# Transposes of new rows one quarter later, products with values two chunks at a time, GpSimd's second rstd before its normalising

## The reference, cut to what matters

```
a = layernorm(x)                                   # per row
q, k, v = a Wq^T, a Wk^T, a Wv^T                   # split into 16 heads of 32
p = softmax(q k^T / sqrt(512) + adj + adj)         # per block and head, 128 x 128
x = x + (p v) Wo^T
b = layernorm(x)
s = softmax(max(b gate_W + gate_b, 1e-4))          # 8 experts, the best two are kept
x = x + sum over the two of weight * (b expert_W[e] + expert_b[e]) / 2
```

## Time and profile before

| what | value |
|---|---|
| median of three executions | 1838.23 us |
| the profiled execution, its own time | 1835.63 us |
| its span in the trace | 1833.7 us |
| TensorE busy | 1658.2 us (90%) |
| VectorE busy | 1277.4 us (70%) |
| ScalarE busy | 985.6 us (54%) |
| GpSimd busy | 985.3 us (54%) |
| TensorE's mean granted clock | 0.96 of full speed |

### The profile page before, as it was taken

The page is one execution under the profiler, slowest core; times in us unless marked ns, Lnnn a source line. Parts: engine busy times, 40 slices in busy tenths (PEclk is TensorE's granted clock), DMA queues, the critical chain, the costliest instruction groups (busy, mean ns, idle before and its releaser), DMA issues. The chain is left out here.

```text
span 1833.7 us, 43506 instructions
## 1 busy us (share of the span) xinstructions
PE 1658.2 (90%) x11856; PEld 1394.6 (76%) x11856; DVE 1277.4 (70%) x4692; ACT 985.6 (54%) x3116; POOL 985.3 (54%) x1722
## 2 busy tenths in 40 slices
PE   4699999999999999999999999998457899999996
PEld 3588788888788887888887888886345678888885
DVE  3467878888878888778888778877543455555554
ACT  3477776677766777766777767767301111111111
POOL 1144555565555555555655555656514456565555
PEclk9899999999999999999999999998669999999998
DMA  5876777777877867777767778766389988888876
GB/s 179 248 212 186 229 230 231 224 236 210 236 229 231 248 201 232 237 224 227 235 202 238 228 228 230 228 201 190 121 278 257 256 163 174 163 166 162 169 157 110
DMA packets 205692, 385.40 MB, mean 210 GB/s; under 512 B 22288, under 2 KB 30480, under 8 KB 205328
## 3 DMA queue, kind: packets, MB, share of 16 engines
q1 hardware_dynamic: 152416, 271.00, 50.3%
q0 software_dynamic: 29680, 69.55, 18.6%
q10 hardware_dynamic: 23360, 42.08, 7.5%
HBM read 206.26 MB, written 176.30 MB: 209 GB/s over the span
## 5 line engine op out<-in xcount | busy, mean ns | idle before, releaser
L593 ACT ACTIVATE prob<-prob,nmax 128x128 f32<-128x128 f32 x1024 | 398.1, 393 | 151.8 <-DVE amax L734 143.7
L983 POOL TENSOR_TENSOR prob<-prob,rinv 128x512 f32<-128x512 f32 x256 | 261.7, 1042 | 254.4 <-DVE rinv L751 254.4
L730 DVE CUSTOM_DVE_ANT_0 prob<-ps_s,bias 128x128 f32<-128x128 f32 x1024 | 237.3, 287 | 163.1 <-PE ps_s L460 117.2
L1190 POOL DMA_INDIRECT out<-yt,token x135 | 211.5, 1566 | 216.0 <-DMA out<-yt,token 72.5
L1126 ACT ACTIVATE xgT_hi<-ps_x 128x512 fp32r<-128x512 f32 x135 | 80.8, 598 | 409.2 <-PE ps_x L1098 330.0
L1110 PE MATMUL ps_y<-we_hi,xgT_hi 128*128 x540 | 227.1, 420 | 21.7 <-DVE xgT_lo L1145 12.3
L1112 PE MATMUL ps_y<-we_hi,xgT_lo 128*128 x540 | 214.8, 398 | 0.0
L1111 PE MATMUL ps_y<-we_lo,xgT_hi 128*128 x540 | 214.6, 397 | 0.0
L631 ACT ACTIVATE pT<-ps_t 128x512 f32<-128x512 f32 x256 | 150.5, 588 | 111.0 <-PE ps_t L469 110.8
L593 ACT ACTIVATION_READ_ACCUMULATOR prob<-prob,nmax 128x1 f32 x1024 | 195.0, 190 | 0.0
L734 DVE TENSOR_REDUCE amax<-prob 128x4 f32<-128x512 f32 x256 | 175.7, 686 | 8.9
(11 more groups left out here) (151 smaller groups left out, 4439.8 us busy)
## 6 DMA issues: line engine op xcount, KB each, us to landing
ks<-kq_parts SPq DMA_DIRECT2D x192, 256.0 KB, 4.3
qs<-kq_parts SPq DMA_DIRECT2D x192, 256.0 KB, 5.5
xg<-x_lists ACTq DMA_DIRECT2D x135, 260.5 KB, 3.6
xin<-x SPq DMA_DIRECT2D x64, 256.0 KB, 6.9
kq_parts<-kT_hi SPq DMA_DIRECT2D x32, 512.0 KB
kq_parts<-kT_lo SPq DMA_DIRECT2D x32, 512.0 KB
kq_parts<-qT_hi SPq DMA_DIRECT2D x32, 512.0 KB
kq_parts<-qT_lo SPq DMA_DIRECT2D x32, 512.0 KB
```

What stands on the lines that cost most here:

```text
L593: last = nc.scalar.activation(prob[:, r, c, h, :], prob[:, r, c, h, :], ACT.Exp, bias=nmax[:, r, i:i + 1], scale=-1.0, accum_out=rsum[:, r ...
L730: last = nc.vector.tensor_tensor_reduce(out=prob[:, r, c, h, :], in0=ps_s[c % 2][:, P * h:P * h + P], in1=bias[:, b % 4, :], scale=-1.0, s ...
L983: tt(prob[:, r, q], prob[:, r, q], rinv[:, r, HC * q:HC * q + HC].unsqueeze(2).to_broadcast([P, HC, P]), ALU.mult)\
L1190: pool.indirect_dma_start(out=out, out_offset=bass.IndirectOffsetOnAxis(ap=token[:, m, :], axis=0), in_=yt[:, r, :], in_offset=None, compu ...
```

## The change

Three edits, all in the order of work of phase A. No operation is added or removed.

1. `small(t, c)`: the transposes of new rows (`X`, parts 0 and 1) of an odd turn stand in quarters 1 and 2 instead of 0 and 1. TensorE, ScalarE and VectorE all follow it.
2. TensorE's `times_v`: instead of one chunk in every quarter, two chunks in quarters 0 and 2 and none in quarters 1 and 3.
3. GpSimd: in an odd turn `second_rstd(t - 3)` stands ahead of `normalise(t, 0)` instead of behind it.

```diff
         def small(t, c):
-            if t % 2 and c < 2:
-                return ("X", t // 2 + 2, c) if okp(t // 2 + 2) else None
+            if t % 2 and c in (1, 2):
+                return ("X", t // 2 + 2, c - 1) if okp(t // 2 + 2) else None
...
                     if ok(t):
                         scores(t, c)
-                    b, cc = (t - 1, c - 1) if c else (t - 2, DC - 1)
-                    if ok(b):
-                        times_v(b, cc)
+                    b, half = (t - 1, 0) if c else (t - 2, 2)
+                    if c % 2 == 0 and ok(b):
+                        times_v(b, half)
+                        times_v(b, half + 1)
                     if ok(t - 1):
                         transpose_probs(t - 1, c)
...
                     if c == 0 and ok(t - 1):
                         normalise(t - 1, 1)
+                    if c == 2 and odd and ok(t - 3):
+                        second_rstd(t - 3)
                     if c == 2 and ok(t):
                         normalise(t, 0)
-                    if c == 2 and odd and ok(t - 3):
-                        second_rstd(t - 3)
```

## The result

The changed kernel takes 1747.11 us (median of four, 1744.31 to 1748.32) against 1836.78 for the kernel before on the same chip: a ratio of 0.9515, 95% interval 0.9495 to 0.9536. Run again, beside runs of its own of the kernel before, it gave 0.9547 (0.9523 to 0.9571). It is faster, as forecast, but by 4.5 to 4.9% and not by the 3.8% of the forecast. The first median lies 3 us under the lower end of the range, the second (1752.23) 2 us above it. In edit 2 alone and in edit 3 alone one execution each ran at a much lower granted clock; it is left out of their times and ratios.

A forecast was written before the change was run, and what follows sets the result against it. TensorE, 90% busy, was taken as the bound. A pair: 38.25 - 1.64 - 0.5 + 0.1 + 0.25, taken as 36.5 us; 27 pairs save 68, five others 1.5, so 1838.2 - 69.5 = 1769 us, range 1750 to 1806.

The forecast's parts named there:

- The stall of O0 and the clock: TensorE in O0: moving the transposes removes the 1.64 us wait for ScalarE's norm and 0.78 of slow clock a pair.
- Rival (b): TensorE's clock stays slow, set off by small new waits: 21 us lost, 1790 us; chance 0.07.
- the same 0.4 us wherever it stands: TensorE's transposes of new rows: each group of four costs 0.4 us in whichever quarter it stands.
- Net for a merge ... I take -0.13: TensorE's values, two chunks together: 0.35 to 0.45 us removed, 0.27 added; -0.13 each, -0.5 a pair with four merges.
- rival (c): TensorE gains more: merges at -1.2 us a pair and no new waits, 35.5 us a pair, 1742 us; chance 0.07.
- The new waits: TensorE waits newly for masks at the end of E0, 0.1 us, and for `kT_lo` in E3, 0.25 a pair.
- rival (e): Queries' HBM round trip makes E0's scores wait, 1865 us at 3.5 us a pair; chance 0.06, two thirds of it slower.
- its chain: GpSimd's earlier rstd frees ScalarE in O3, brings `oT_lo` up to 0.8 us earlier, cutting E3's new wait by 0.2 to 0.3.
- the row of `comb_k`: VectorE's two-input operation took 0.19 us beside GpSimd's rstd, so small rstd operations should not hold VectorE back.
- the other five pairs: Phase A pairs outside the 27: no such stall, 0.3 us each from the merges, 1.5 us in all.
- (a): VectorE becomes the bound through waits for ScalarE's copies or GpSimd holds: 37.5 us a pair, 1797 us; chance 0.12.
- (d): TensorE's wait for the norm only moves to O1: 1830 to 1838 us, no change; chance 0.03.

The follow-up runs named there:

- edit 2 alone: Only the values order changed (two chunks together in quarters 0 and 2), against the kernel before: 1809.8 us, ratio 0.9881.
- edit 3 alone: Only GpSimd's order changed (second rstd ahead of normalising in odd turns), against the kernel before: 1830.8 us, ratio 0.9996.
- Edit 1 alone: Only the transposes of new rows moved one quarter later, against the kernel before: 1766.31 us, ratio 0.9661.
- edits 2 and 3: Values merged and GpSimd's rstd moved, transposes of new rows left in place, against the kernel before: 1787.82 us, ratio 0.9761.
- edits 1 and 2: Transposes of new rows moved and values merged, GpSimd's order left as it was, against the kernel before: 1757.74 us, ratio 0.9586.
- the first profile: The changed kernel with all three edits, first measurement, against the kernel before: 1747.11 us, ratio 0.9515.
- the second profile: The changed kernel run again unchanged, beside new runs of the kernel before: 1752.23 us, ratio 0.9547.
- The groups apart: Changed kernel with the transposes of probabilities between the two groups of values in quarters 0 and 2: 1802.69 us, ratio 0.9841 to the kernel before.
- Fewer bytes: Changed kernel with the third load of each stack bringing a quarter of its bytes from block 2 on: 1738.83 us, ratio 0.9487 to the kernel before.

## Why the prediction was right or wrong

**The stall of O0 and the clock: right in mechanism, 0.2 us too small.** Edit 1 alone removed the wait and all slow stretches. Before, 12 of the 27 stalls had one behind them, 1.55 us each, which is 0.69 of the 0.78 a pair. In the 27 pairs of all profiles here such stretches came only behind stalls, the shortest of 1.41 us (edit 2 alone), but far from behind each: 4 in 27 with edit 2 alone, 1 in 27 with edits 2 and 3, and none behind one of 2.11 us with edits 1 and 2. What decides it, no run shows. The two that are left in the first profile follow waits of 1.54 and 2.16 us before the scores:

```profile
921.30 0.63 PE L460 MATMUL ps_s<-ks,qs 96*128 96x128 f32 x4 [2.16 <-issue]
921.87 1.08 PE L480 MATMUL ps_o<-pT,vv 128*32 128x128 f32 x16
```

The group of 16 lasts 1.08 us here and 0.64 in other pairs: 1.2 GHz instead of 2.4. Rival (b), that the small new waits keep the clock slow, is out at its price: two stretches, and none in the second profile. The sum missed that the transposes behind the stall cost 0.66 and not 0.43 ("the same 0.4 us wherever it stands"), 6 us in 27 pairs.

**"Net for a merge ... I take -0.13": this term was mis-sized.** The size is -0.27. The quarter that loses a group loses 0.48 us, not 0.35 to 0.45, and the second group adds 0.21, not 0.27. Edit 2 alone shows both numbers. The groups apart show the other side: a second group that does not touch the first costs its quarter 0.51 (E2 takes 4.60 with one group, 5.11 with two apart). Over four merges that is 1.1 us a pair instead of 0.5, 15 us in 27 pairs. The prediction had the 0.3 at the end of its bound and gave it to rival (c) with 0.07. Leaving the column groups and coming back once more costs 0.29 us, by the groups apart. Going from one group of matmuls to another is not what costs: from scores straight to transposes it is 0.48 us, four steps of 0.12. The Trainium skill's rule (TensorEngine Tiling (Array Packing), Key Properties), that TensorE drains where the tiling mode is switched, agrees with that in sign and gives no size.

**The new waits: right in place for two, wrong in size, and one missed; they hid the merges.** From bare work the pair comes to 39.03 - 0.78 - 1.64 - 0.22 - 1.08 = 35.3 us; the pair at 556.6 took 35.40. The mean is 36.31, so the waits and their clock cost 1.0, not the 0.35 of the sum. By quarters, against the shortest of each: E3 (`kT_lo`) 0.33, near the 0.25 taken; E0 0.26, of which two slow stretches are about a half, against 0.1 (0.25 in the second profile, without any slow stretch); O3, which ends with the scores' wait for the queries, 0.35, against nothing. That last is rival (e), which the prediction held to eat a part of the gain at most. Its slack was worked out as 0.6 to 1.9 less up to 1; it measured 2.22 before and 0.39 after. The prediction let the store come 1.4 us later against O1; in the mean of the 27 pairs it stood 2.0 us ahead of O1 and now stands 0.5 behind. Fewer bytes brought the slack back to 1.4 and took 0.4 us off a pair. So beside edit 1 the merges' 1.1 us of bare work gave only 0.2 to 0.3 a pair (36.65 to 36.42, and 36.55 to 36.31 or 36.37 with edit 3). That is what the sum took for merges and waits together, 0.5 less 0.25: two errors of 15 and 17 us cancelled, by luck.

**Edit 3: its chain is there, but not what won here.** ScalarE's second norm waits no more. Alone, edit 3 takes the hold on line 816 from 1216 to 850 ns. But edit 1 alone takes it to 871, and edits 1 and 2 together to 875, so behind them edit 3 adds only 0.05 to 0.09 us (785, and 821 in the second profile). And the fall of `dlt` is edit 1's: 176 ns with it alone, 201 with edits 1 and 2. What edit 3 does move is `e_lo`, and with it the hold, from line 799 in edits 1 and 2 to line 792 in all three:

```profile
L799 DVE TENSOR_TENSOR key<-eq,const 128x16 f32<-128x16 f32 x27 | 29.9, 1107 | 0.9
L817 DVE TENSOR_TENSOR em<-eexp,mask 128x16 f32<-128x16 f32 x27 | 23.6, 875 | 0.0
```

```profile
L792 DVE TENSOR_TENSOR eq<-score,m 128x16 f32<-128x16 f32 x27 | 32.9, 1219 | 0.0
L817 DVE TENSOR_TENSOR em<-eexp,mask 128x16 f32<-128x16 f32 x27 | 21.2, 785 | 0.0
```

The small rstd operations held nothing back, as the row of `comb_k` had it: its mean is 192 ns before and after. The Trainium skill (SBUF — State Buffer, Who interferes with whom) says that a VectorE instruction with two SBUF inputs contends with a GpSimd one that reads SBUF. This case's large operations agree: `eq` (line 792) has a mean of 1219 ns under `e_lo`, and 143 where it ran free in the kernel before; the small ones do not.

**Outside the pairs: the step that failed.** The sum gave 1.5 us to the other five pairs and, without a reason, nothing to the rest; the first profile gives 16.0. Of the 89.4 us of the span, 4.5 came before the first scores (edit 1; the three kernels without it start at 63.3 to 65.6, those with it at 56.5 to 59.5), 3.8 in the five pairs, 3.5 between the last scores and phase B (edit 3), and 4.2 in phase B, which is no work of the change: the same code took 6.4 us more in the next profile. There the span is 82.5 us shorter than before: 7.0 at the start, 71.6 in the 27 pairs, 2.6 in the five, 3.5 at the tail and 2.2 lost in phase B. So start and tail, 8.0 and 10.5 us, come back and phase B does not. Why edit 1 starts sooner is not traced to its end; one wait of the first projections for the low part of new rows, 5.0 us before, is 1.4 now.

**The sum.** 69.5 forecast; 89.4 in the profile. The 20 us between are: 5.2 in the 27 pairs (merges +15 and transposes +6, new waits about -17, rounding), 4.5 at the start, 2.3 in the other pairs, 3.5 at the tail and 4.2 that are spread of phase B, with some tenths of rounding. So the mechanism inside the pairs held, and 14.5 of the 20 us are what the sum left out outside the 27 pairs; the rest is in the main the transposes behind the stall. Whether the median falls 3 us below the range or just into it is within the spread of phase B, and so luck. Rivals (a), (d) and the slower part of (e) did not come, and of (c) the merges did, but with waits. Two slips of the working matter little: by its own terms O0 is 4.8 us and not 4.7 (it took 4.47), and rival (e) at 3.5 us is 1863.5 and not 1865.

## What to carry to other kernels

Price a switch between a full-array matmul and a column-grouped one by what the next quarter without it looks like, not by its own duration: two groups put side by side saved about 0.3 us each time here. When a stall goes, count what follows it as well, the slow clock and the lost overlap, and then look at every transfer with a round trip: the slack of each shrinks by the time won, and here that of the queries, with VectorE's `kT_lo`, set the new limit. Look at what an edit does at the start and at the end of the pipeline too: 8 us of this gain lay there. Small reorderings of GpSimd's stream have worth only with the collisions that they move on VectorE, and can be nothing alone.

## What the runs showed of the hardware

A VectorE operation on 16 columns took 1219 ns in the mean instead of 143 because it started just behind a GpSimd operation of 1.3 us, and it ended with it:

```profile
665.20 1.27 POOL L1021 TENSOR_TENSOR e_lo<-e_stage,e_hi 128x512 fp32r<-128x512 f32 x1 [2.28 <-ACT e_hi L648]
...
665.30 1.22 DVE L792 TENSOR_TENSOR eq<-score,m 128x16 f32<-128x16 f32 x1
```

Such a hold under `e_lo` comes in 25 to 27 of the 27 pairs of every kernel here, on whichever small operation happens to stand there. With one SBUF input, `tensor_scalar` was held too (0.77 us under the normalising, with the groups apart; 0.18 to 0.30 in the mean where it ran mostly free). And the same transfers, asked for in another order, took 6.6 or 8.6 us from the first issue to the last landing.
